# Loading the first attention group during the projections, and storing the last projections during the attention

## The reference

```python
x = x + attention(layernorm(x))      # latent attention, 16 heads of 32, rope parts of 16
x = x + ffn(layernorm(x))            # gate, up, silu, down; blockwise FP4 of x, h and the weights

# attention, of the normalised x
c_q, c_kv = x @ W_DQ, x @ W_DKV                  # 128 latent features each
Q = concat(c_q @ W_UQ, rope(c_q @ W_QR))         # per head 32 + 16
K = concat(c_kv @ W_UK, rope(x @ W_KR))          # the rope key is shared by all heads
V = c_kv @ W_UV
weights = softmax(causal(clip(Q @ K.T, -80, 80)) / sqrt(48))
return (weights @ V) @ W_O
```

## Time and profile before

| | us |
|---|---|
| median of 3 runs (lowest, highest) | 3091.75 (3090.26, 3096.07) |
| the profiled execution's own time | 3095.26 |
| span of its profile | 3093.5 |

### The profile page before, as it was taken

How to read it: one execution, slowest core, us unless ns; L and a number is a source line. 1 busy time by engine, 2 the same in 40 slices (tenths; PEclk the granted TensorE clock), 3 DMA queues, 4 the chain that set the end, 5 groups by cost and what they waited for, 6 DMA issues and landing times.

```text
span 3093.5 us, 65827 instructions
## 1 busy us (share of the span) xinstructions
PE 2989.5 (97%) x23204; PEld 2208.2 (71%) x23204; DVE 2614.2 (85%) x4257; ACT 1306.2 (42%) x1946; POOL 743.8 (24%) x664
## 2 busy tenths in 40 slices
PE   8999699999999999979999999999999999999999
PEld 6777444444444444468888888888888888888887
DVE  8999578888888888878888888888888888888886
ACT  4455367877777777732222222222222222222221
POOL 2434200000000000013333333333333333333332
PEclk9999899999999999989999999999999999999999
DMA  6888856656656655531111111111111111111110
GB/s 230 280 286 276 242 125 144 140 135 139 152 130 142 143 135 139 140 123 42 33 36 41 41 41 41 41 33 36 41 41 41 41 41 35 37 38 41 41 35 14
DMA packets 251213, 304.22 MB, mean 98 GB/s; under 512 B 25552, under 2 KB 158544, under 8 KB 251088
## 3 DMA queue, kind: packets, MB, share of 16 engines
q1 hardware_dynamic: 251088, 302.89, 35.8%
HBM read 190.35 MB, written 112.46 MB: 98 GB/s over the span
## 4 chain that ended last, share of the span: by engine, by line
PE 53%; DVE 3%; issue 1%; ACT 0%; DMA 0%; DVEq 0%; POOL 0%; SPq 0%; ACTq 0%
PE p_ring L1743 19%; PE p_ring L1771 15%; PE ps_od L1743 10%; PE ps_od L1723 5%; PE p_ring L1761 2%; PE p_ring L1751 1%; DVE sb_fp_tmp L102 1%; DVE sb_wg_lo L1649 0%; PE ps_od L1771 0%; DVE sb_h_amax L88 0%; DVE sb_stage L1620 0%; PE p_ring L1723 0%; DVE sb_xq L1601 0%; PE p_ring L1786 0%; DVE sb_xq L1595 0%
## 5 line engine op out<-in xcount | busy, mean ns | idle before, releaser
L940 ACT ACTIVATE sb_probs<-scores 128x1024 f32<-128x1024 f32 (+3 forms) x768 | 590.2, 814 | 221.3 <-PE scores L1144 215.2
L1012 DVE TENSOR_SCALAR sb_probs<-sb_probs 128x2048 f32<-128x2048 f32 (+3 forms) x320 | 289.7, 905 | 100.0 <-ACT sb_probs L940 100.0
L679 POOL TENSOR_TENSOR sb_at_in<-sb_at_in,sb_inv_in 128x512 f32<-128x512 f32 x64 | 85.5, 1335 | 1081.3 <-DMA sb_inv_in<-dinv 1080.6
L1159 PE MATMUL ps_od<-sb_probs,sb_v 128*32 128x512 f32 (+3 forms) x3072 | 328.2, 499 | 2.8 <-DVE sb_probs L1004 1.5
L1446 POOL TENSOR_TENSOR sb_stage<-sb_stage,sb_h_inv 128x512 f32<-128x512 f32 (+1 forms) x192 | 210.5, 1096 | 359.4 <-DVE sb_h_inv L94 359.4
L1743 PE MATMUL p_ring<-sb_wg_hi,sb_xq_hi 128*128 128x512 f32 (+1 forms) x1024 | 294.8, 369 | 0.3 <-DVE sb_wd_lo L1649 0.3
L1743 PE MATMUL p_ring<-sb_wg_lo,sb_xq_hi 128*128 128x512 f32 (+1 forms) x1024 | 290.9, 365 | 0.0
L1743 PE MATMUL p_ring<-sb_wg_hi,sb_xq_lo 128*128 128x512 f32 (+1 forms) x1024 | 290.0, 364 | 0.0
L1144 PEld LDWEIGHTS scores<-sb_q_hi,sb_k_hi 32*128 32x128 f32 x1536 | 73.7, 182 | 300.2 <-ACT sb_probs L940 257.2
L1771 PE MATMUL p_ring<-sb_wd_hi,sb_ht_hi 128*128 128x512 f32 x693 | 275.8, 398 | 0.0
L1771 PE MATMUL p_ring<-sb_wd_hi,sb_ht_lo 128*128 128x512 f32 x693 | 270.3, 390 | 0.0
(11 more groups left out here) (193 smaller groups left out, 6645.8 us busy)
## 6 DMA issues: line engine op xcount, KB each, us to landing
kq<-sb_kq_out SPq DMA_DIRECT2D x32, 1024.0 KB, 6.6
sb_kq_raw<-kq SPq DMA_DIRECT2D x64, 512.0 KB, 10.1
sb_xin<-in_L_attn_x_dram SPq DMA_DIRECT2D x32, 512.0 KB, 5.4
rq<-sb_r_out SPq DMA_DIRECT2D x64, 256.0 KB, 2.9
v<-sb_v_out SPq DMA_DIRECT2D x64, 256.0 KB, 3.6
sb_qr<-rq SPq DMA_DIRECT2D x256, 64.0 KB
sb_kr_hi<-kr SPq DMA_DIRECT2D x32, 512.0 KB
sb_kr_lo<-kr SPq DMA_DIRECT2D x32, 512.0 KB
```

Of the source, the lines that this page charges most:

```text
L940: act.activation(probs[:, k % PROBS, 2 * pair:2 * pair + 2, off:BANK], scores[(2 * k + pair) % RING2][:, :, off:BANK], ACT.Exp, scale=SCAL ...
L1012: i = dve.tensor_scalar(pr, pr, P_MAX, P_MIN, ALU.min, ALU.max)
L1159: mm = pe.matmul(ps_o[rows, off:BANK], v_sb[s][:, j, rows], probs[:, k % PROBS, i, off:BANK], start=(j == 0), stop=last)
```

## The change

- A class Front owns the buffers that live through both stages: group 0's kq_raw, qr, kr_hi, kr_lo, v, and also r_out, v_out and the weight-piece buffers. Group 0's 13 loads are issued by SyncE in the projections, at the beginning of body 14, after a wait for the stores of sequence 0.
- The last half takes its units in the order C0, C1, KR, R, K0, K1, Q0, Q1, V0, V1. TensorE waits for C1's rests before R. ScalarE rounds KR's sum after R and R's sum after K1. DVE does the weight piece after R.
- SyncE ends the last half after kr and kq. The stores of rq, v and wq of body 15 are issued at the start of the attention block, and the waits at the end of the projections are gone.
- In the attention ScalarE waits for `stored[0]` before step 1 of the first group and for `stored[1]` before step 3; SyncE waits for both before group 1's 11 loads. probs slots 4 and 5 lie in r_out, `added` in v_out, the weight piece in the projections' buffers.

```diff
-UNITS1_LAST = [u for u in UNITS1 if u[0] != "X"]
+UNITS1_LAST = ["C0", "C1", "KR", "R", "K0", "K1", "Q0", "Q1", "V0", "V1"]
...
+class Front:
...
+    def store_rope(self, sp, b, half):
+        cols = slice(half * BANK, (half + 1) * BANK)
+        for s in range(2):
+            for c in range(2):
+                sp.dma_start(self.rq_v[s, c, b, :, :, cols], self.r_out[:, half, s, c]).then_inc(self.stored[half], 16)
...
+    def load_raw(self, sp, g):
+        for k in range(2):
+            sp.dma_start(self.kq_raw[:, k], self.t["kq"][k, bass.ds(g * NI, NI)].rearrange("i p t -> (i p) t")
+                         ).then_inc(self.raw_loaded, 16)
+
+    def load_group(self, sp, g, it2, done, qr, kr_hi, kr_lo, v):
+        def get(dst, src):
+            sp.dma_start(dst.bitcast(F32), src).then_inc(done, 16)
+
+        for i in range(NI):
+            for hl in range(2):
+                get(qr[DH * i + DR * hl:DH * i + DR * hl + DR], self.t["rq"][hl, g * NI + i])
+        for hl, kr in enumerate((kr_hi, kr_lo)):
+            get(kr[:], self.t["kr"][hl, it2].unsqueeze(0).to_broadcast([P // DR, DR, S]))
+        sp.dma_start(v[:], self.t["v"][g].rearrange("(k p) d -> p k d", p=P)).then_inc(done, 16)
...
@@ projections, SyncE
+                if is_last(b) and not last:
+                    for h in range(2):
+                        sp.wait_ge(stored[h], 2 * STORES1)
+                    front.load_raw(sp, 0)
+                    front.load_group(sp, 0, 0, front.loaded[0], front.qr, front.kr_hi, front.kr_lo, front.v)
                 sp.wait_ge(rope_lo, n * 2 + 2 + 1)
...
+                if last:
+                    return
                 sp.wait_ge(piece_done, n + 1)
-                sp.dma_start(t["wq_all"][n], piece_y[:]).then_inc(piece_stored, 16)
+                front.store_piece(sp, n)
...
             blocks(sp, body)
-            sp.wait_ge(piece_stored, 16 * (2 * B + 1))
-            for h in range(2):
-                sp.wait_ge(stored[h], STORES1 * (B + 1))
...
@@ projections, ScalarE
-                    if name == "K1":
+                    if name == ("R" if last else "K1"):
                         act.wait_ge(rope_sum, n * 2 + 1)
...
-                    if name == "V1":
+                    if name == ("K1" if last else "V1"):
                         act.wait_ge(rope_sum, n * 2 + 2)
...
@@ projections, DVE
-                    if name == ("KR" if last else "X1"):
+                    if name == ("R" if last else "X1"):
                         dve.wait_ge(piece_loaded, n * 16 + 16)
...
@@ projections, TensorE
                     elif name == "R":
+                        if last:
+                            freed_last(pe, n, "C1")
...
@@ attention, SyncE
-            load_raw(0, 0)
-            load(0, 0)
+            front.store_rope(sp, B - 1, 1)
+            front.store_values(sp, B - 1, 1)
+            front.store_piece(sp, 2 * B - 1)
+            load_raw(0, 1)
             load_piece(0)
-            load_raw(0, 1)
+            for h in range(HALF):
+                sp.wait_ge(front.stored[h], half_stored)
             load(0, 1)
...
@@ attention, ScalarE, before the exponentials of step k
+                if first and k == FIRST_HALF_SLOT:
+                    act.wait_ge(front.stored[0], half_stored)
+                if first and k == LAST_HALF_SLOT:
+                    act.wait_ge(front.stored[1], half_stored)
                 act.wait_ge(pv_done, number + 1)
...
@@ attention, DVE, step 11 of the first group
+                        if first:
+                            dve.wait_ge(front.piece_stored, 16 * (2 * B + 1))
```

More of the change, by code:

```diff
@@ L122, in projections @@
+def projections(nc, t, B, front):
     with ExitStack() as ctx:
@@ L182, in projections @@
         rope_lo = sem("rope_lo")
-        stored = [sem(f"stored{h}") for h in range(2)]
+        stored = front.stored
         piece_loaded = sem("piece_loaded")
@@ L275, in body @@
                     sp.dma_start(piece_in[:], t["w_all"][n + 1]).then_inc(piece_loaded, 16)
+                if last:
+                    return
                 sp.wait_ge(piece_done, n + 1)
[L277 removed]
+                front.store_piece(sp, n)
                 sp.wait_ge(rope_lo, n * 2 + 2 + 2)
[L279 to L281 removed]
+                front.store_rope(sp, b, half)
                 freed(sp, n, "V1")
[L283 to L285 removed]
+                front.store_values(sp, b, half)
             blocks(sp, body)
[L288 to L290 removed]
         @block.gpsimd
@@ L547, in body @@
                     elif name[0] in "KQ":
-                        if name in ("K0", "Q0"):
+                        if name in ("K0", "Q0") and not (last and name == "Q0"):
                             (freed_last if last else freed)(pe, n, "C0" if name == "K0" else "C1")
@@ L692, in load_job, with attention @@
         sp.dma_start(to[:, 0:w], self.mats[m][r * P:(r + 1) * P, a:a + w]).then_inc(self.loads[slot_of(n)], 16)
-def attention(nc, t, B, ahead):
+def attention(nc, t, B, front, ahead):
     with ExitStack() as ctx:
@@ L704, in attention @@
         ps_o, ps_d = ahead.ps_od[:, 0, :], ahead.ps_od[:, 1, :]
[L707 to L718, removed]
+        bound = sb("bound", [P, P])
+        ones = sb("ones", [P, DH])
+        split0 = [sb(f"{x}0", [P, S], F32R) for x in ("k_hi", "k_lo", "q_hi", "q_lo")]
+        split1 = [sb(f"{x}1", [P, S], F32R) for x in ("k_hi", "k_lo", "q_hi", "q_lo")]
+        low_probs = sb("probs", [P, PROBS - 2, NI, BANK])
+        high_probs = front.r_out.rearrange("p h s c t -> p h (s c) t")
+        k_hi, k_lo, q_hi, q_lo = ([split0[x], split1[x]] for x in range(4))
+        kq_raw = front.kq_raw
+        qr = [front.qr, sb("qr1", [P, S], F32R)]
+        kr_hi = [front.kr_hi, sb("kr_hi1", [P, S], F32R)]
+        kr_lo = [front.kr_lo, sb("kr_lo1", [P, S], F32R)]
+        v_sb = [front.v, sb("v1", [P, S // P, P])]
+        added = front.v_out
         o_sb = sb("o", [P, HALF, BANK])
         d_sb = sb("d", [P, BANK])
-        bound = sb("bound", [P, P])
-        ones = sb("ones", [P, DH])
         WP = t["w_all"].shape[-1]
[L725 to L731, removed]
+        w_in, w_sb, w_big, w_tmp = front.piece_in, front.piece_y, front.piece_big, front.piece_tmp
+        w_amax, w_scale, w_inv = front.piece_amax, front.piece_scale, front.piece_inv
         w_loaded = sem("w_loaded2")
@@ L740, in attention @@
         s_cst = sem("cst")
-        raw_loaded = sem("raw_loaded")
+        raw_loaded = front.raw_loaded
         raw_rounded = sem("raw_rounded")
         raw_split = sem("raw_split")
-        loaded = [sem(f"group_loaded{s}") for s in range(2)]
+        loaded = front.loaded
+        half_stored = STORES1 * (B + 1)
         sc_ready = sem("sc_ready")
@@ L758, in attention, with probs @@
         G2 = 2 * B
+        def probs(k):
+            k = k % PROBS
+            return low_probs[:, k] if k < PROBS - 2 else high_probs[:, k - (PROBS - 2)]
         def groups(eng, body):
@@ L1001, in clip @@
                 if j >= 4 * half:
-                    pr = probs[:, k % PROBS, :, off:off + P]
+                    pr = probs(k)[:, :, off:off + P]
                     i = dve.scalar_tensor_tensor(out=pr, in0=pr, scalar=P_MIN,
@@ L1022, in add_up @@
                 heads = slice(2 * pair, 2 * pair + 2)
[L1023 removed]
+                dve.tensor_tensor(added[:, n, heads], probs(a)[:, heads], probs(b)[:, heads],
                                   ALU.add).then_inc(summed, 1)
@@ L1158, in weigh @@
                     rows = slice(DH * i, DH * i + DH)
-                    mm = pe.matmul(ps_o[rows, off:BANK], v_sb[s][:, j, rows], probs[:, k % PROBS, i, off:BANK],
+                    mm = pe.matmul(ps_o[rows, off:BANK], v_sb[s][:, j, rows], probs(k)[:, i, off:BANK],
                                    start=(j == 0), stop=last)
@@ L1171, in denominators @@
                     pe.wait_ge(clipped, step_no(it2, s, k) + 1)
-                    src, off = probs[:, k % PROBS], STEPS[k][2]
+                    src, off = probs(k), STEPS[k][2]
                 start = n in (0, DENOMS_HALF)
@@ L1830, in latent_attention_block @@
              dinv=scratch("dinv", (2 * B, P, CHUNK)), wq_all=scratch("wq_all", w_all.shape))
-    projections(nc, t, B)
     with ExitStack() as ctx:
-        ahead = Ahead(nc, ctx, t)
-        attention(nc, t, B, ahead)
+        with ExitStack() as front_ctx:
+            front = Front(nc, front_ctx, t)
+            projections(nc, t, B, front)
+            ahead = Ahead(nc, ctx, t)
+            attention(nc, t, B, front, ahead)
         feed_forward(nc, t, B, ahead)
```

61 lines of the change are left out of this document (38 added, 23 removed).

## The result

The changed kernel took 3068.76 us (median of 4 runs, 3064.62 to 3076.94), the kernel before 3093.91 us beside it (4 runs, 3090.26 to 3100.59): a ratio of 0.9917 with a 95% interval of 0.9901 to 0.9932, 25 us less. The forecast was 3070.5 in a range of 3059 to 3078.

What follows compares the result with a forecast made beforehand. TensorE, busy in 97% of the span, was taken to bound the kernel, its standstill between projections and attention to be shortened: 22.7 - 1.5 = 21.2 us off 3095.26 gives 3074.1, with the median 3.5 lower at 3070.5, range 3059 to 3078.

Steps and rivals of the forecast that it cites:

- The load of group 0: In the projections' last batch: 3.15 MB cost 16 us of queue, landing near 347 us, ending the 17.5 us sb_v wait.
- The piece it pushes back: DVE's next weight piece, behind group 0's loads on the queue, lands at 354.6, wanted at about 347.3; DVE's work takes 5.5.
- The end of the block: End of the projections: the block ends at 360.1 through DVE's late piece, and the attention starts at 360.6, not 369.58.
- The rope unit early: Last half of the projections: R's products done by 347.3, ScalarE's copies by 355.9, TensorE's matmuls still ending at 353.25.
- The first scores: Start of the attention: first scores near 365 instead of 391.4, 26.4 us earlier, perhaps at the full clock.
- The waits that take their place: First attention steps: last v store lands about 375, w_in at 379.7; step 2 weighed at 381.4, saving 22.7 us.
- The half clock: After TensorE stands some 6 us before weighing step 2, a lowered clock costs 0 to 3.9 us, taken as 1.5.
- The sum: Whole kernel: 22.7 - 1.5 = 21.2 us off the profiled 3095.26, giving 3074.1, and 3070.5 for the median.
- A: Rival: the queue holds nothing up and the piece comes in time; first scores at 360.7, 3058 to 3061 us; chance 0.24.
- B: Rival: unequal rings, group 0 costs 19.8 us, everything late moves 3.8, half clock costs 3.9; saving 15, 3077; chance 0.16.
- C: Rival: slower, w_in landing after 402.4 if group 0 costs 38.7 us among stores; 3098 at 45 us; chance 0.03.
- D: Rival: group 0 has not landed when the block ends, first scores still wait for sb_v; time 3090; chance 0.03.

Runs made afterwards that it cites:

- e10: The changed kernel measured once more, unaltered, on a third chip; ratio 0.9908 to the kernel before.
- e6: The changed kernel with one unused 2.1 MB copy added right behind group 0's early loads on the same queue; ratio 0.9932 to the kernel before.
- e13: The changed kernel with SyncE issuing the 13 early loads only behind kr, kq, the weight piece and wq of half 14; ratio 0.9928 to the kernel before.
- e4: The changed kernel with w_in issued ahead of the last stores and group 1's kq_raw rounded 4 steps later; ratio 0.9910 to the kernel before.
- e7: The changed kernel with the 13 early loads issued by ScalarE between its units of half 14; ratio 0.9896 to the kernel before, median 3067.22 us.
- e9: The changed kernel with the 13 early loads one sequence earlier (half 12), that sequence written out instead of looped; ratio 1.0086 to the kernel before.
- e12: The changed kernel with the early loads on ScalarE's queue and w_in issued first in the attention; ratio 0.9910 to the kernel before.
- e3: The changed kernel with w_in issued first in the attention, ahead of the last stores; ratio 0.9921 to the kernel before.
- e5: The changed kernel with early load and tail change undone, only buffers and the code around them moved; ratio 0.9986 to the kernel before.
- e11: The changed kernel with ScalarE issuing the early loads in the changed kernel's order, not before some 328 us; ratio 0.9901 to the kernel before.
- the tail alone: The changed kernel with the early load undone: group 0's 13 loads issued at the attention's start, ahead of the last stores; ratio 0.9934 to the kernel before.

## Why the prediction was right

*The load of group 0* lands in the projections and the wait for sb_v is gone, as forecast. Its cost on the queue was taken as 16 us. The piece it pushes back was forecast for 354.6 and came at 355.6; e10 had 354.4. DVE's work on it took the 5.5 us of the forecast. e6 shows the mechanism: 2.1 MB more move the piece by 5.5 us. The sum of the queue's work held as well: the last v store was forecast for about 375, and SyncE's wait for the stores was over at 377.1.

*The end of the block* was mis-sized: forecast 360.6, measured 363.5, and its cause was not the forecast's. DVE's late piece is real (361.1), but SyncE was later (363.1). The working counted SyncE's issues at the durations of the earlier trace rows and left out that issues take longer behind so much data: the kr stores 7.78 us for four. e13 takes the piece's delay away and the block ends no earlier.

*The rope unit early* did as worked out: R's products until 347.05 (347.3), ScalarE's last copy at 355.14 (355.9), no wait of TensorE.

*The first scores* came 4.2 us after the attention's first instruction: 367.7 against 365, the lateness of the block. They ran at the full clock up to the wait at 375.8, as the forecast thought possible. That was in part luck: in e4, with the same code on TensorE, the clock was back at 0.50 between 369.8 and 371.8, 6 to 8 us after the first scores, and so it was in e6, e7, e9, e12 and e13.

*The waits that take their place* were the right ones. w_in came at 382.9, forecast 379.7, and step 2 was weighed at 385.35, forecast 381.4. e3 corrects the reason: the forecast named DVE's wait for w_in alone as the last one, but ScalarE's for kq_raw of group 1 (7.1 us) held the steps just as long, and the working has no such wait. Both kq_raw and w_in stand behind the last stores, so that the number survived. The half clock was taken as 1.5 us: from step 2 to group 1 were 18.4 us before, 19.6 in the changed kernel, so 1.2.

*The sum* was 21.2 us against 18.3 in the profiled executions. It is made of 17.6 at the seam, forecast 21.2. The rest is no effect that the forecast named, and the medians differ by 25. Of the difference e5 shows 4 us that come with the moved buffers and code, and the interval of the ratio is 4.8 us wide to either side; more I can't settle. So it was in part luck that the median came near the forecast. It has two errors in it that cancel: a seam saving 3.6 us too large, and some 4 us (if e5's holds here too) from moved buffers and code, a cause that was put at nothing. And the kernel before, which the forecast took at 3091.75, stands at 3093.91 with its fourth run, which hides 2 us of the difference.

*The rivals.* A (nothing held up) is out: both pieces of data were late. B (unequal rings) gave 15 us for the profiled execution, and 18.3 lie midway between it and the forecast. B's 3.8 us of lateness came true in size: step 2 was 4.0 us later than forecast. Its cause did not: a group that costs 19.8 us would have brought the piece at 358.4 and not at 355.6, and 2.9 of the 4.0 us were there when the block ended, behind SyncE's issues. The forecast says that the landing of kq_raw and w_in within 0.5 us agrees with order on each ring and no order across them. The row bears out only the second: kq_raw, issued later, was not later to land. No row here shows the order on a ring. C would have needed 38.7 us for group 0. D is out: the first scores wait for no load.

## What to carry to other kernels

Work moved off the critical path onto a DMA queue is paid for by whatever stands behind it there: list what is issued later on the same queue, and who waits for it. Count the issuing engine too, since its issues stretch behind megabytes of loads, even if another engine issued the loads. Issued by a second engine with time to spare, the loads left step 2 5 us (e11) and 10 us (e7) earlier, but the time could not be told from the changed kernel's. Before adding a second part to a change, measure the first alone: here the tail alone had 20 of the 25 us. When one of two waits that end together is removed, nothing happens (e3), and two remedies that share a resource don't add up (13.5 and 9.3 gave 17.6).

## What the runs showed of the hardware

- Four kr stores that SyncE issues in 1.75 us in the kernel before took 7.78 us behind 3.15 MB of loads on its queue. With these loads on ScalarE's queue SyncE was held up too: four v stores took 7.67 us (e7) and 7.93 (e11), not 2.8 to 3.7.
- With one loop pass written out ahead of the attention (e9), a loop with unchanged code came with instruction fetches, 76 packets against none between 500 and 1200 us, and with up to 7.7 us more in every second group. The ratio went from 0.992 to 1.009.
- TensorE stood from 375.8 to 382.9; its clock was 0.50 from 377.8 to 387.6, so also in the 4.7 us after it worked again.
- Directly after the warm-up matmuls the clock is not settled. In the changed kernel it was 1.00 from the first scores to the wait 8 us later; in e4, with the same code on TensorE, it rose to 1.00 and was back at 0.50 between 6 and 8 us after the first scores.
